# One more drain in GpSimd's program, ahead of the last expert's scatters

## The chip, the cores and the metric

The kernel runs on one core of one Trainium2 chip. The metric is device time in microseconds (us); lower is better. A core has five engines that run their own instruction streams: TensorE (PE; its weight loads are PEld), VectorE (DVE), ScalarE (ACT), GpSimd (POOL) and SyncE (SP). They meet only at semaphores. A "q" behind an engine's name (POOLq) marks instructions of its sequencer: waits, branches and drains. A drain is an instruction without data that stands in an engine's program and is meant to let what was issued before it finish; TensorE's at the close begins at 898.2 us in this trace, takes 4.27 us, and ends when the last matmul does, at 902.4.

## The reference

A token-shift layer whose channel mix goes through 16 experts; B = 8, T = 1024, D = 512, F = 1024, E = 16, N = 8192 tokens, C = 512 places for each expert.

```
xprev = concat([cond[:, None], x[:, :-1]], 1)
xk = x + (xprev - x) * maa_k ;  xr = x + (xprev - x) * maa_r
expert = token_id * 5099 % 16 ; pos = rank of the token within its expert
slot = expert * C + pos, tokens with pos >= C are dropped
h = relu(expert_in @ w_key[e]) ** 2 ;  y = h @ w_value[e]
out = x + sigmoid(xr @ w_recept) * y[slot]
```

## The kernel before

Phase 1 computes the gates sigmoid(xr @ w_recept) for 16 groups of 512 tokens and stores them to the DRAM tensor `gates`; beside it the routing is worked out: for each of the 64 tiles of 128 slots, which token stands in each row (`row_tok`), and the rows of the pairs (`row_pair`). Phase 2 goes through the 16 experts. For each, TensorE makes 8 tiles of the hidden layer (`up`, 4 steps of depth) and then 4 tiles of 128 rows of the result (`down`, 8 steps of depth). Each float32 product is made as three products of split operands (`triple`, lines 758 to 760). ScalarE and VectorE split, apply relu and square. VectorE closes each result tile t with two operations: `gate` = acc x mask x gate (line 682) and `xrow` = gate + xrow (line 685), which raises s_res.

GpSimd issues every indirect DMA, in an order written out by hand (lines 368 to 389). `gather_pairs(e)` fetches the inputs of expert e in 16 DMAs (line 348); `gather_gate` and `gather_cur` fetch for each tile the gate rows and the x rows (both through line 330); `scatter(e, t)` waits for s_res (line 354) and writes the tile's rows to `out` (line 355). In the loop over experts, the pairs of expert e + 2 come first, and then, for each tile, the scatter of expert e and the gathers of expert e + 1. For e = 14 there are no pairs left; its last instruction is the gather of x rows for tile 3 of expert 15 (line 387). For e = 15 only the four scatters remain. The loop at line 388 then waits until each tile's scatters have all landed. In all GpSimd issues 448 indirect DMAs. SyncE issues all other DMAs.

The block that holds the five programs closes at its end; the profile puts the instructions of this close under line 81. Each engine runs a drain there and then passes a meeting of semaphores with the others. These drains are not written in the kernel's text: they come with the block.

Of the kernel before, what the change touches and what calls it, by code (L numbers as in the profile page):

```python
# [23 lines left out]
def moe_token_shift(nc, x, pairs, xs_t, ids, maa_k, maa_r, w_recept_t, w_key, w_value, out, gates):  # L24
# [23 lines left out]
    E, D, F = w_key.shape  # L48
# [32 lines left out]
    with ExitStack() as ctx:  # L81
# [216 lines left out]
        def _(pool):  # L298
# [29 lines left out]
            def gather(table, e, t, rows, dst, s):  # L328
                a = e * ST + t
                pool.indirect_dma_start(dst, None, table,  # L330
                                        bass.IndirectOffsetOnAxis(rows[:, a:a + 1], 0)).then_inc(s, 16)

            def gather_cur(e, t):
                if e > 0:
                    pool.wait_ge(s_scat[t], 16 * e)
                gather(x, e, t, row_tok, xrow[:, t, :], s_cur[t])

            def gather_gate(e, t):
                if e > 0:
                    pool.wait_ge(s_res, (e - 1) * ST + t + 1)  # L340
                gather(gates, e, t, row_tok, gate[:, t, :], s_gat[t])

            def gather_pairs(e):
                if e >= 2:
                    pool.wait_ge(s_block, 2 * KD * (e - 1))
                for i in range(SB):
                    a = e * SB + i
                    pool.indirect_dma_start(pair[e % 2][:, i, :], None, pairs,  # L348
                                            bass.IndirectOffsetOnAxis(row_pair[:, a:a + 1], 0)).then_inc(
                                                s_pair[e % 2], 16)  # L350

            def scatter(e, t):
                a = e * ST + t
                pool.wait_ge(s_res, e * ST + t + 1)
                pool.indirect_dma_start(out, bass.IndirectOffsetOnAxis(row_tok[:, a:a + 1], 0),  # L355
                                        xrow[:, t, :], None).then_inc(s_scat[t], 16)
# [20 lines left out]
            for e in range(E):  # L377
                if e + 2 < E:
                    gather_pairs(e + 2)
                for t in range(ST):  # L380
                    scatter(e, t)
                    if e + 1 < E:
                        gather_gate(e + 1, t)
                        if t > 0:
                            gather_cur(e + 1, t - 1)
                if e + 1 < E:
                    gather_cur(e + 1, ST - 1)
            for t in range(ST):
                pool.wait_ge(s_scat[t], 16 * E)

# [501 lines left out]
```

## Time and profile before

| | |
|---|---|
| median of 3 runs | 918.49 us (917.84 to 919.08) |
| span of the profiled execution, first to last instruction | 916.6 us |
| the profiled execution's own time | not given beside the span |
| PE busy | 893.0 us (97%) |
| DVE busy | 775.1 us (85%) |
| POOL busy | 550.8 us (60%) |
| ACT busy | 380.0 us (41%) |
| granted TensorE clock, mean share of full speed | 0.988 |

Busy time is the sum of an engine's instructions; drains, waits and branches are not counted in it. The span is what one profiled execution shows; the median is from other executions.

### The profile page before, as it was taken

What the parts mean: (1) busy time and instruction counts of PE and PEld (TensorE: products, weight loads), DVE (VectorE), ACT (ScalarE), POOL (GpSimd) and SP (SyncE); (2) the same over time, 40 slices, a digit from 0 to 9 for tenths busy, and PEclk for the clock granted to TensorE, in tenths of its full rate; (3) what the DMA queues carried; (4) which work ended last, traced back from release to release, by engine and by line L of the source; (5) the groups of instructions that cost most, each with busy time, mean ns of one, the idle gap of its engine ahead of it and who ended that gap; (6) DMA issues with size and microseconds to landing.
All of it is one profiled execution on the core that took longest, in us unless ns stands there. A gap on an engine that the chain in (4) does not pass through costs nothing.

```text
span 916.6 us, 10890 instructions
## 1 busy us (share of the span) xinstructions
PE 893.0 (97%) x3915; PEld 735.4 (80%) x3915; DVE 775.1 (85%) x1060; ACT 380.0 (41%) x582; POOL 550.8 (60%) x485
## 2 busy tenths in 40 slices
PE   6999999999999999999999999999999999999993
PEld 5788878888888888888888888888888888888882
DVE  6999986878898989898989898989888898989841
ACT  4444322545352625353444444343525262535320
POOL 5222203576777777677767777677777676770601
PEclk9999988999999999999999999999999999999997
DMA  9555634866666666667585848485766667673600
GB/s 329 203 177 190 204 118 141 295 210 228 206 223 210 211 225 220 230 194 249 172 274 175 269 148 286 143 280 166 255 189 237 206 213 224 214 237 106 230 12 34
DMA packets 73765, 186.40 MB, mean 203 GB/s; under 512 B 11760, under 2 KB 11760, under 8 KB 73712
## 3 DMA queue, kind: packets, MB, share of 16 engines
q1 hardware_dynamic: 46064, 101.80, 34.0%
q0 software_dynamic: 27648, 83.91, 26.7%
q8 instruction: 31, 0.51, 0.2%
q14 instruction: 22, 0.18, 0.1%
HBM read 152.11 MB, written 33.55 MB: 203 GB/s over the span
## 4 chain that ended last, share of the span: by engine, by line
PE 94%; DVE 2%; issue 1%; DMA 0%; POOL 0%; ACT 0%; SPq 0%; DVEq 0%; POOLq 0%
PE acc L758 31%; PE acc L760 31%; PE acc L759 31%; PE rt_bank L792 2%; DVE xr_lo L636 1%; DMA wr_raw<-w_recept_t 0%; DVE mix L627 0%; DVE mix L630 0%; DVE cum L517 0%; POOL out L355 0%; DVE onehot L511 0%; DVE id_low L509 0%; DVE totals L521 0%; PE rt_bank L801 0%; DVE gate L682 0%
## 5 line engine op out<-in xcount | busy, mean ns | idle before, releaser
L758 PE MATMUL acc<-xk_hi,wk_hi 128*128 128x512 f32 x512 | 199.5, 390 | 0.0
L760 PE MATMUL acc<-xk_hi,wk_lo 128*128 128x512 f32 x512 | 199.4, 390 | 0.0
L759 PE MATMUL acc<-wv_lo,h_hi 128*128 128x512 f32 x512 | 199.3, 389 | 0.0
L760 PE MATMUL acc<-wv_hi,h_lo 128*128 128x512 f32 x512 | 199.2, 389 | 0.0
L758 PE MATMUL acc<-wv_hi,h_hi 128*128 128x512 f32 x512 | 199.2, 389 | 0.0
L759 PE MATMUL acc<-xk_lo,wk_hi 128*128 128x512 f32 x512 | 199.2, 389 | 0.0
L433 ACT ACTIVATE hid<-acc 128x512 f32<-128x512 f32 x128 | 76.6, 599 | 266.1 <-PE acc L760 266.1
L348 POOL DMA_INDIRECT pair_even<-pairs,row_pair x128 | 140.1, 1095 | 70.6 <-issue 38.7
L348 POOL DMA_INDIRECT pair_odd<-pairs,row_pair x128 | 140.1, 1095 | 46.6 <-issue 38.7
L355 POOL DMA_INDIRECT out<-xrow,row_tok x64 | 84.9, 1327 | 111.8 <-DVE xrow L685 102.1
L670 DVE TENSOR_TENSOR hid<-hid 128x512 f32<-128x512 f32 x128 | 88.4, 690 | 51.6 <-ACT hid L433 49.8
L760 PEld LDWEIGHTS acc<-xk_hi,wk_lo 128*128 128x128 f32 x512 | 96.1, 188 | 20.3
L759 PEld LDWEIGHTS acc<-xk_lo,wk_hi 128*128 128x128 f32 x512 | 96.1, 188 | 20.2
L758 PEld LDWEIGHTS acc<-wv_hi,h_hi 128*128 128x128 f32 x512 | 96.1, 188 | 20.0
L760 PEld LDWEIGHTS acc<-wv_hi,h_lo 128*128 128x128 f32 x512 | 96.1, 188 | 20.0
L758 PEld LDWEIGHTS acc<-xk_hi,wk_hi 128*128 128x128 f32 x512 | 96.1, 188 | 20.0
L759 PEld LDWEIGHTS acc<-wv_lo,h_hi 128*128 128x128 f32 x512 | 96.1, 188 | 20.0
L758 PE MATMUL acc<-wr_hi,xr_hi 128*128 128x512 f32 x256 | 101.8, 397 | 7.9 <-DVE xr_lo L636 7.9
L759 PE MATMUL acc<-wr_lo,xr_hi 128*128 128x512 f32 x256 | 101.1, 395 | 0.0
L760 PE MATMUL acc<-wr_hi,xr_lo 128*128 128x512 f32 x256 | 100.9, 394 | 0.0
L330 POOL DMA_INDIRECT xrow<-x,row_tok x64 | 79.5, 1242 | 21.2 <-issue 18.0
L674 DVE TENSOR_TENSOR h_lo<-hid,h_hi 128x512 fp32r<-128x512 f32 x128 | 87.9, 687 | 1.4
(105 smaller groups left out, 1259.1 us busy)
## 6 DMA issues: line engine op xcount, KB each, us to landing
raw<-w_key SPq DMA_DIRECT2D x64, 512.0 KB, 4.4
raw<-w_value SPq DMA_DIRECT2D x64, 512.0 KB, 3.9
xT<-xs_t SPq DMA_DIRECT2D x64, 256.5 KB, 4.0
gates<-gate SPq DMA_DIRECT2D x64, 256.0 KB, 2.8
pair_even<-pairs,row_pair POOLq DMA_INDIRECT x128, 3.3
pair_odd<-pairs,row_pair POOLq DMA_INDIRECT x128, 3.0
wr_raw<-w_recept_t SPq DMA_DIRECT2D x4, 256.0 KB, 5.0
xrow<-x,row_tok POOLq DMA_INDIRECT x64, 5.2
```

What stands on the lines that cost most here:

```text
L330: pool.indirect_dma_start(dst, None, table, bass.IndirectOffsetOnAxis(rows[:, a:a + 1], 0)).then_inc(s, 16)
L348: pool.indirect_dma_start(pair[e % 2][:, i, :], None, pairs, bass.IndirectOffsetOnAxis(row_pair[:, a:a + 1], 0)).then_inc(s_pair[e % 2], 16)
L355: pool.indirect_dma_start(out, bass.IndirectOffsetOnAxis(row_tok[:, a:a + 1], 0), xrow[:, t, :], None).then_inc(s_scat[t], 16)
L433: act.activation(hid[:, n % H_SLOTS, :], acc[n % 4][:, :], ACT.Relu).then_inc(s_relu, 1)
L636: dve.tensor_tensor(xr_lo[:, g % 2, k, :], mix[:, n % MIX_SLOTS, :], xr_hi[:, g % 2, k, :].bitcast(F32), ALU.subtract).then_inc(s_rlo, 1)
L670: dve.tensor_tensor(h, h, h, ALU.mult).then_inc(s_sq, 1)
L674: dve.tensor_tensor(h_lo[:, n % KF, :], hid[:, n % H_SLOTS, :], h_hi[:, n % KF, :].bitcast(F32), ALU.subtract).then_inc(s_hlo, 1)
L758: pe.matmul(bank[:, :], hi, m_hi, start=first, stop=False)
L759: pe.matmul(bank[:, :], hi, m_lo, start=False, stop=False)
L760: return pe.matmul(bank[:, :], lo, m_hi, start=False, stop=last)
L792: mm = pe.matmul(inv_ps[:, 0:2 * A], oh_b[:, :, j], oh_aw[:, :, :, j].rearrange("p h a -> p (h a)"), start=(j == 0), stop=(j == J - 1))
```

## The change

A drain is issued on GpSimd once, at the end of the loop's turn e = 14. It stands behind the gather of line 387 and ahead of the wait and the scatter of tile 0 of expert 15. Nothing else is changed.

```diff
                 if e + 1 < E:
                     gather_cur(e + 1, ST - 1)
+                if e + 2 == E:
+                    pool.drain()
             for t in range(ST):
                 pool.wait_ge(s_scat[t], 16 * E)
```

Blank lines of the diff are left out here; they put the drain on line 391 of the changed file.

## Rows read from the trace of the kernel before

**Rows 1.** The page: busy time with share and count, and the chain by engine.
```profile
PE 893.0 (97%) x3915; PEld 735.4 (80%) x3915; DVE 775.1 (85%) x1060; ACT 380.0 (41%) x582; POOL 550.8 (60%) x485
...
PE 94%; DVE 2%; issue 1%; DMA 0%; POOL 0%; ACT 0%; SPq 0%; DVEq 0%; POOLq 0%
```

**Rows 2.** Timeline, PE and DVE, 901.7 to the end: start us, us, what.
```profile
901.99 0.39 PE L760 MATMUL acc<-wv_hi,h_lo 128*128 128x512 f32 x1
...
902.41 0.75 DVE L682 SCALAR_TENSOR_TENSOR gate<-acc,mask,gate 128x512 f32<-128x512 f32 x1 [3.96 <-PE acc L760]
903.20 0.69 DVE L685 TENSOR_TENSOR xrow<-gate,xrow 128x512 f32<-128x512 f32 x1
```

**Rows 3.** Timeline, POOL, expert 15's scatters after the first; idle time in brackets.
```profile
893.29 0.99 POOL L355 DMA_INDIRECT out<-xrow,row_tok  x1 [4.45 <-DVE xrow L685]
898.73 0.97 POOL L355 DMA_INDIRECT out<-xrow,row_tok  x1 [4.46 <-DVE xrow L685]
904.17 0.97 POOL L355 DMA_INDIRECT out<-xrow,row_tok  x1 [4.47 <-DVE xrow L685]
```

**Rows 4.** Line 389: duration ns min/median/max, first and last start us.
```profile
L389 POOLq EVENT_SEMAPHORE  x2: 17/30/43, 903.9 to 906.9; - x2
```

**Rows 5.** Line 81, the block's close, same columns.
```profile
L81 POOLq EVENT_SEMAPHORE  x2: 17/17/17, 916.4 to 916.5; - x2
L81 SPq DRAIN  x1: 123/123/123, 864.8 to 864.8; - x1
L81 ACTq DRAIN  x1: 652/652/652, 882.0 to 882.0; - x1
L81 PEldq DRAIN  x1: 4267/4267/4267, 898.2 to 898.2; - x1
L81 DVEq DRAIN  x1: 730/730/730, 903.2 to 903.2; - x1
...
L81 POOLq DRAIN  x1: 9214/9214/9214, 907.2 to 907.2; - x1
L81 SPq EVENT_SEMAPHORE  x1: 17/17/17, 916.5 to 916.5; - x1
```

**Rows 6.** Busy us by stretch: PE, PEld, DVE, ACT, POOL, PEclk, DMA share, GB/s.
```profile
868.40:887.90 19.50, 19.50 (x87) 16.14 (x86) 11.62 (x16) 7.80 (x13) 0.10 (x2) 1.00 0.05 17
...
907.10:916.40 9.30, 0.00 (x0) 0.00 (x0) 0.00 (x0) 0.00 (x0) 0.00 (x0) 0.52 0.00 0
```

**Rows 7.** DMA in 907.2 to 916.4.
```profile
DMA packets 0, 0.00 MB, mean 0 GB/s; under 512 B 0, under 2 KB 0, under 8 KB 0
```

**Rows 8.** Line 884, the program's start, GpSimd: columns as in rows 4.
```profile
L884 POOLq DRAIN  x1: 188/188/188, 0.4 to 0.4; - x1
L884 POOL MEMSET const-uint8-127<- x1: 119/119/119, 0.4 to 0.4; 128x1 uint8 x1
```

**Rows 9.** Lines 348, 330 and 355: all indirect DMAs, and line 330's landings.
```profile
L348 POOL DMA_INDIRECT pair_even<-pairs,row_pair x128: 942/1028/1913, 149.0 to 759.1; - x128
L348 POOL DMA_INDIRECT pair_odd<-pairs,row_pair x128: 942/1027/1911, 184.7 to 803.9; - x128
...
L330 POOL DMA_INDIRECT xrow<-x,row_tok x64: 942/972/1795, 171.2 to 866.8; - x64
L330 POOL DMA_INDIRECT gate<-gates,row_tok x64: 944/1081/1209, 211.2 to 864.1; - x64
...
DMA to landing us min/median/max: 3.5/4.7/7.0
...
L355 POOL DMA_INDIRECT out<-xrow,row_tok x64: 966/1072/1730, 239.5 to 904.2; - x64
```

**Rows 10.** Timeline, POOL, around the place of the change.
```profile
865.54 0.95 POOL L330 DMA_INDIRECT xrow<-x,row_tok  x1 [0.30 <-issue]
866.80 1.66 POOL L330 DMA_INDIRECT xrow<-x,row_tok  x1 [0.30 <-issue]
887.85 0.99 POOL L355 DMA_INDIRECT out<-xrow,row_tok  x1 [19.40 <-DVE xrow L685]
```

## The prediction

> **What bounds the kernel now.** I read the busy times first, then the chain that ended last, then the ends of the engines. PE is busy 893.0 of 916.6 us, and the chain is 94% PE [rows 1]. So nothing in GpSimd's program matters until PE stops, unless it makes PE wait; what GpSimd does matters after PE's last product. The reader should therefore look at the last 15 us. The last matmul begins at 901.99, the last pair of VectorE operations runs from 902.41 to 903.89, and the last scatter is issued at 904.17 and takes 0.97 [rows 2, 3]. GpSimd's last wait, for that scatter's landing, is done at 906.9 [rows 4]. The span still ends only at 916.6.
>
> The program's end accounts for what is left. Every engine has a drain at line 81, where the block closes. Sync, ScalarE, TensorE and VectorE have begun theirs by 903.2, and the longest of these, TensorE's 4,267 ns from 898.2, ends at 902.4, with its last matmul. GpSimd's begins at 907.2 and takes 9,214 ns. The closing semaphore instructions start at 916.4 and 916.5, right behind it [rows 5]. All four others wait for GpSimd there, so these 9.21 us, 1.0% of the span, are the last thing on the path. They are no wait for transfers or compute: in 907.1 to 916.4 no engine is busy and the DMA share is 0.00 [rows 6], and in 907.2 to 916.4 the count of packets is 0 [rows 7]. So this drain does work of its own, on something GpSimd has piled up. The only other GpSimd drain in the trace, at 0.4 us, took 188 ns [rows 8]. It has memsets ahead of it and no indirect DMA; one such memset takes 119 ns [rows 8], so most of the 188 is a wait for it. Between the two drains lie 448 indirect DMAs (128 + 128 pair gathers, 64 + 64 row gathers, 64 scatters) [rows 9]. My reading is that a GpSimd drain has one piece of bookkeeping for each software DMA issued since the drain before: (9,214 - 188) / 448 = 20.1 ns each with a fixed 188, or 9,214 / 448 = 20.6 ns each with nothing fixed.
>
> **The change part by part.** One instruction is added, on GpSimd alone, when e is 14: after the last gather of the last expert (line 387) and ahead of the wait and scatter (lines 354 and 355) of tile 0 of expert 15. Nothing is removed or moved. There are four terms.
>
> 1. The added drain. It stands behind 444 of the 448 DMAs. I price it at 444 x 20.6 ns = 9.13 us. The trace has no drain of GpSimd in mid-program, so the bounds are 0.19 us (the early drain, rows 8) and 9.21 us (the late one, rows 5), plus at most a wait for the gathers still in flight. I take 9.13 because the place resembles the late drain in all but 4 DMAs. What hides it is GpSimd's idle time: its last gather is issued from 866.80 to 868.46, and the scatter behind it begins at 887.85, after 19.40 us of idle time that VectorE's xrow operation ended [rows 10]. Even if the drain first waits for the transfers in flight, these land by 7.0 us after issue at most [rows 9], which is 873.8, counted from the start of the issue; the drain then ends near 882.9, about 5 us before the scatter is due. During the gap the DMA share is 0.05 [rows 6]. Cost: 0.
>
> 2. What is queued behind it: only the four scatters and their final waits. The gathers that VectorE's results need were issued ahead of it, and PE and ScalarE wait for nothing that GpSimd still issues. If the cover were gone the scatters could still catch up. They are paced by PE, 5.44 us apart (887.85, 893.29, 898.73, 904.17), but one takes 0.97 to 0.99 and about 0.30 lies between issues [rows 3, 10]. Three go by in 3 x 1.29 = 3.9 us, so the first could start at 904.17 - 3.87 = 900.3 without moving the last. The real cover is 900.3 - 868.5 = 31.8 us, more than three times the price.
>
> 3. The final drain, now with 4 DMAs since the one before. By count alone it is 4 x 20.6 ns = 0.08 us; with the early drain's 188 ns as a fixed part, 0.27 us. The bounds are 0.08 and 9.21. I take 0.2, nearest to the early drain, because the scatters have landed and there is nothing else to wait for. It saves 9.21 - 0.2 = 9.01 us, all of it exposed. Behind it the 0.2 us of closing semaphores, 916.4 to 916.6, stays.
>
> 4. One more instruction to fetch and decode, in an idle engine: 0, bounded by the 0.30 us between two issues [rows 10], and it is under the same gap.
>
> In sum the span goes from 916.6 to 916.6 - 9.0 = 907.6. The profile gives the execution's span and no time beside it; the median of the three timed runs is 918.49, 1.89 us above. That difference lies around the span and stays. Forecast: 918.49 - 9.0 = 909.5 us, 0.98% faster. What is late next is the last product with its evict, scatter and landing, which no drain touches.
>
> A rule of the Trainium skill speaks against this. VectorE: DVE Perf Modes, section The DRAIN you can't avoid, says that besides VectorE's pipeline flush there are boilerplate drains in the preamble and postamble, constant at about 12 ns on all five engines. Priced so, the final drain would hold nothing to move, the added one would be free, and the time would stay 918.5. The trace disagrees for GpSimd: 188 and 9,214 ns [rows 5, 8]; Sync's 123 ns is no 12 ns either [rows 5].
>
> **The rivals.**
>
> A. A fixed price: a GpSimd drain costs about 9.2 us once the program has used software DMAs at all, whatever their number, as if it walked a table of fixed size. For it: the trace has only one such drain, and one point makes no line. Against it: nothing but the plainness of a count. The added drain is then hidden (868.5 + 9.2 = 877.7, before 887.85) and the final one stays 9.21: 918.5 us, no change. That the added drain doesn't do the same work as the one at the block's end, or that the work is tied to the program's end, gives the same time.
>
> B. Partly fixed: say half of the 9.21 is fixed, half goes by count. The final drain is then 4.6 + 0.0, the saving 4.6 us, and the time 913.9 us.
>
> C. Slower: in mid-program the drain handles each DMA at a much dearer price, because it must ask after each one while traffic is on. The place is GpSimd between 868.5 and the last scatter. At 100 ns each it takes 44.4 us and ends at 912.9; the last scatter starts 3.9 later, at 916.8 in place of 904.17, which is 12.6 us late, and with 9.0 saved at the end the time is 918.49 + 12.6 - 9.0 = 922.1 us. It decides from 31.8 + 9.0 = 40.8 us of drain, or 92 ns for each DMA, 4.5 times what the final drain shows. Against it: the gap is nearly without traffic [rows 6].
>
> **How the numbers follow.** Forecast 0.79, A 0.12, B 0.05, C 0.04. A measurement of this kernel tells 0.2%, 1.84 us, from no change. Faster: forecast and B, 0.84. Same: A, less a small part of it, 0.11. Slower: C and that part, a disturbance I don't see, 0.05. The forecast's own spread is 0.08 to 0.27 for the last drain and 0.6 us of the runs to either side (917.84 to 919.08): 908.8 to 910.2. The range reaches part of B: 908.5 to 913.0, which leaves out A, C and half of B, under 2 in 10.
>
> **What would show it.** In the profile after: a GpSimd drain at line 391 (the changed file's), from about 868.6 and 9.1 us long (5 us more if it waits for landings first); the drain at line 81 down from 9,214 to between 80 and 300 ns; scatters at unchanged times, 887.85 and so on; the chain up to the last landing unchanged; the span at 907.6. The forecast is wrong if the drain at line 81 stays at 9.2 us (A) or near 4.6 (B), or if the first scatter of expert 15 is released by the drain and not by VectorE (towards C). One thing the result alone can't tell: a cost that is paid once, by whichever drain comes first after a software DMA, gives the same time as a cost by count.

## The result, and the profile after

The changed kernel takes 910.12 us (median of 4 runs, 909.66 to 910.77) against 918.4 us before (median of 4 runs, 917.84 to 919.08). The ratio is 0.9908, 95% interval [0.9896, 0.992]: 0.92% faster. The forecast was 909.5. In experiments 1 to 4 and 9 to 12, further down, the chips granted TensorE a lower mean clock (0.949 to 0.989) and times ran up to 995 us, so of these only ratios of fast runs and the lengths of GpSimd's drains are compared.

The profile of one execution (909.74 us, of which 908.0 are the span) shows where it went. First the added drain at line 391 (the columns are duration in ns min/median/max, first and last start in us), then line 81, the block's close:

```profile
L391 POOLq DRAIN  x1: 11235/11235/11235, 866.4 to 866.4; - x1
```

```profile
L81 PEldq DRAIN  x1: 4267/4267/4267, 898.4 to 898.4; - x1
L81 DVEq DRAIN  x1: 732/732/732, 903.5 to 903.5; - x1
...
L81 POOLq DRAIN  x1: 383/383/383, 907.4 to 907.4; - x1
L81 SPq EVENT_SEMAPHORE  x1: 17/17/17, 908.0 to 908.0; - x1
```

The close of [rows 5] fell from 9,214 to 383 ns, 8.83 us. The timeline of GpSimd shows that the added drain delayed no scatter:

```profile
867.05 1.66 POOL L330 DMA_INDIRECT xrow<-x,row_tok  x1 [0.30 <-issue]
888.11 0.99 POOL L355 DMA_INDIRECT out<-xrow,row_tok  x1 [19.40 <-DVE xrow L689]
...
904.42 0.97 POOL L355 DMA_INDIRECT out<-xrow,row_tok  x1 [4.48 <-DVE xrow L689]
```

The gap of 19.40 us is the one of [rows 10] to the hundredth, and VectorE still ends it. The drain's own row needs care. It starts at 866.4, when the last gather has not begun (867.05), so 2.3 of its 11.2 us pass before that gather's issue has ended. It ends at 877.6, which is 8.9 us behind the end of the last gather's issue at 868.7 and 10.5 us ahead of the scatter.

The last scatter begins at 904.42 where it began at 904.17 [rows 3], so 8.83 - 0.25 = 8.58 us is what the span shows (916.6 to 908.0). Those 0.25 us come from earlier: the last matmul starts at 902.24 where it started at 901.99 [rows 2]. That looks like spread and not like the change: experiments 7 and 8 below hold the same drain, and there the last scatter begins at 903.95 and 904.56, to either side of both kernels.

### The profile page after: what moved, and what is told of

It reads as the page before. It is cut to its first block, busy times and chain, and to the rows that moved or that the text cites. A ratio compares the mean times of both kernels' runs of the same rounds, so it can differ in the third digit from the quotient of the medians.

```text
span 908.0 us, 10891 instructions
## 1 busy us (share of the span) xinstructions
PE 893.5 (98%) x3915; PEld 735.7 (81%) x3915; DVE 775.2 (85%) x1060; ACT 380.0 (42%) x582; POOL 549.4 (61%) x485
## 4 chain that ended last, share of the span: by engine, by line
PE 95%; DVE 2%; issue 1%; DMA 0%; POOL 0%; ACT 0%; SPq 0%; DVEq 0%; POOLq 0%
PE acc L762 31%; PE acc L764 31%; PE acc L763 31%; PE rt_bank L796 2%; DVE xr_lo L640 1%; DMA wr_raw<-w_recept_t 0%; DVE mix L631 0%; DVE mix L634 0%; DVE cum L521 0%; POOL out L355 0%; DVE onehot L515 0%; DVE id_low L513 0%; DVE totals L525 0%; PE rt_bank L805 0%; DVE gate L686 0%
```

## The experiments

What had to be told apart: my theory (work for each DMA since the last drain, here about 20 ns) from a cost that the first drain behind a software DMA pays once, and from a price that is partly fixed; then, whether the cover is what makes the added drain free. The lengths of GpSimd's drains hold from run to run: 383 ns came out twice, and the early drain of [rows 8] took 188 or 189 ns in every run. The edits of experiments 7, 8 and 12 are shown against the changed kernel, all others against the kernel before; blank lines are left out.

### 1 and 11. One drain, early

```diff
                     gather_cur(e + 1, ST - 1)
+                if e == 0:
+                    pool.drain()
```

> The changed kernel's two drains can be read in two ways: a cost by count, or a cost that the first drain behind a software DMA pays once. Here the only added drain stands at the end of e = 0, behind 68 DMAs, and 380 follow it. By count, with the line through the two measured closes (9,214 ns for 448 DMAs, 383 ns for 4: 19.9 ns each and 303 ns fixed), the added drain takes 68 x 19.9 + 303 = 1.66 us and the close 380 x 19.9 + 303 = 7.86 us; the time is 918.4 - 1.35 = 917.05 us. Paid once: the added drain takes about 9 us, the close 0.2 to 0.4, and the time is that of the changed kernel, 909.5 to 910. By a table of fixed size (rival A), already contradicted by the 383 ns: both 9.2 us, 918.4.

The close, in the first and in the repeated run:

```profile
L81 POOLq DRAIN  x1: 9203/9203/9203, 919.9 to 919.9; - x1
```

```profile
L81 POOLq DRAIN  x1: 9203/9203/9203, 933.0 to 933.0; - x1
```

The ratio to the kernel before is 0.9994 [0.9914, 1.0074]. A cost paid once is out: the close is as dear as without the drain. But so is my line of 19.9 ns: 380 DMAs cost what 448 do, to 11 ns. There is an upper limit of some kind; experiments 2, 9 and 10 show that it is a peak to which the cost returns. The repeat was for the time:

> The kernel with one drain at the end of e = 0 once more, to have its time to a few tenths of a per cent. In its first run the close took 9,203 ns behind 380 DMAs, 11 ns less than with 448. So no change: 918.4 to 918.7 us, within 0.2% of the kernel before. By the line of 19.9 ns each it would be 917.1; by a cost paid once, 910.

The repeat gave the length again, and no time that tells 0.2%: 944 to 991 us, beside 934 to 988 for the kernel before. Its time stays unmeasured; that the close is unchanged is shown.

### 2. One drain, half way

```diff
                     gather_cur(e + 1, ST - 1)
+                if e == 7:
+                    pool.drain()
```

> The only added drain stands at the end of e = 7, behind 40 + 8 x 28 = 264 DMAs; 184 follow it. By count: the close takes 184 x 19.9 + 303 = 3.96 us, the time is 918.4 - 5.25 = 913.15 us. Paid once: close 0.2 to 0.4 us, time 909.5 to 910. A half-fixed price (rival B) would leave the close near 4.6 + 1.9 = 6.5 us and the time near 915.7.

```profile
L81 POOLq DRAIN  x1: 6917/6917/6917, 929.2 to 929.2; - x1
```

6.92 us, where the line gives 3.96 and rival B 6.5. B looks right for a moment, but a fixed half can't be reconciled with the changed kernel's 383 ns for 4 DMAs. Ratio 0.9986 [0.9891, 1.0081]; the 2.3 us that the close lost are below what it tells.

### 3. Many drains

```diff
+            pool.drain()
             pool.wait_ge(s_rows, 1)
             gather_pairs(0)
...
                     scatter(e, t)
+                    if e == 15 and t == 2:
+                        pool.drain()
...
                     gather_cur(e + 1, ST - 1)
+                if e in (0, 2, 6, 13, 14):
+                    pool.drain()
+                if e == 14:
+                    pool.drain()
```

> Nine drains besides the close, each with another count since the one before: 0 DMAs behind GpSimd's 18 subtractions and the constants of phase 1; 68 at the end of e = 0; 56 at e = 2; 112 at e = 6; 196 at e = 13; 12 at e = 14 and 0 right behind it; 3 behind the third scatter of expert 15; 1 at the close. By count of DMAs, from the end of the last issue: 0.2 to 0.3 us for 0, then 1.66, 1.42, 2.53, 4.20, 0.54, 0.3, 0.36, and 0.32 for the close. By count of all instructions the first would take 36 x 19.9 ns more, about 1.0 us. If a drain waits until transfers in flight have landed, each in mid-program stays at least 3 to 7 us behind its last issue. The time: all of it in GpSimd's idle time, so that of the changed kernel, 910.1, within 0.6; slower if GpSimd, which runs ahead of VectorE by little at some of these places, delays a gather.

The rows of the drain behind phase 1's subtractions, of the second one at e = 14, and of the close:

```profile
L367 POOLq DRAIN  x1: 1456/1456/1456, 115.3 to 115.3; - x1
...
L394 POOLq DRAIN  x1: 53/53/53, 887.1 to 887.1; - x1
...
L81 POOLq DRAIN  x1: 128/128/128, 922.8 to 922.8; - x1
```

The first has only to outlast a subtraction that is issued at 115.32 and takes 1.36 us; it ends at 116.75, 0.07 us behind it. So compute instructions leave no work that shows, DMAs do. A drain right behind another takes 53 ns, and one DMA takes the close to 128 ns. The five drains at line 392 have gathers in flight in front of them and run from 3.0 to 9.2 us behind the last issue. For 12 DMAs it is 3.0 us (887.1 against 884.07, the end of the last issue). The trace's last landing update is at 886.56, 0.5 us before that drain's end; behind the third scatter, where 3 DMAs are counted, the last landing is at 917.05 and the drain ends at 917.21. So a short drain waits for the landing, and drains with transfers in flight are unfit for the law; hence experiments 9 and 10. The edit adds eight drains; the nine of the expectation take in the close. Ratio 0.9868 [0.9748, 0.9988]: they cost nothing that can be seen, though those at e = 0, 2 and 6 hold up the next pair gathers, which start 0.73 us behind the drain's end.

### 4. The changed kernel again

> The changed kernel again, for comparison on the same chip: 910.1 us, 0.991 of the kernel before; the drain at e = 14 ends 8.9 us behind the last gather's issue, the close takes 0.38 us, by every theory.

Ratio 0.9909 [0.9825, 0.9992], close 383 ns, and the added drain ends 8.89 us behind the last issue. The time in us was 928.43 on this chip.

### 5. The drain without its cover

```diff
                     scatter(e, t)
+                    if e == 15 and t == 2:
+                        pool.drain()
```

> The same one drain, moved out of its cover: it stands behind the third scatter of expert 15 and ahead of the fourth. 447 DMAs stand before it. If place and cover are what matters, it takes 447 x 19.9 = 8.9 us, plus up to 0.3, from the end of the third scatter's issue at 899.7, so to 908.6 to 908.9, and the fourth scatter starts there in place of 904.2, 4.4 to 4.7 us late; the close has one DMA and takes 0.32 us, 8.9 us less. Time 918.4 + 4.5 - 8.9 = 914.0 us. If a drain anywhere ahead of the close shortened the program as such: 910.

914.89 us against 918.71, ratio 0.9956 [0.9939, 0.9973], so 3.8 us of the 9 remain. GpSimd's timeline, and the close:

```profile
899.95 0.97 POOL L355 DMA_INDIRECT out<-xrow,row_tok  x1 [4.45 <-DVE xrow L687]
910.79 0.97 POOL L355 DMA_INDIRECT out<-xrow,row_tok  x1 [9.87 <-issue]
```

```profile
L81 POOLq DRAIN  x1: 138/138/138, 913.8 to 913.8; - x1
```

In place of "<-DVE xrow" stands "<-issue": nothing but the drain held the fourth scatter. By the spacing of 5.44 us it was due at 905.39 and began at 910.79, 5.4 late; 9.21 - 0.14 - 5.4 = 3.7 us, as timed. I had 4.5 late; the drain ended 9.1 us behind the issue and 0.7 more passed until the scatter, as it does in the other runs that have a ready DMA right behind a drain (0.73 to 0.76 us, once 1.05). What counts is the cover, not the drain.

### 6. The drain behind the last scatter

```diff
                     scatter(e, t)
+                    if e == 15 and t == 3:
+                        pool.drain()
```

> The drain stands behind the fourth scatter of expert 15, ahead of the waits for its landing. All 448 DMAs are before it and one of them is in flight. If the drain does its work by count while the last transfer flies, it runs from 905.1 to 905.1 + 8.9 = 914.0, the waits are then already met, the close takes 0.3 us, and the time is 918.4 - 9.2 + (914.0 - 907.0) + 0.3 = 916.5 us: 1.9 us faster, the flight of the last scatter. If a drain first waits for the landing (906.9) and then does its count, the time is 918.4 plus 0.3, no change.

917.26 us against 918.71, ratio 0.9983 [0.9974, 0.9993]. The scatter, the drain, and the wait behind it:

```profile
905.04 0.97 POOL L355 DMA_INDIRECT out<-xrow,row_tok  x1 [4.47 <-DVE xrow L687]
...
L383 POOLq DRAIN  x1: 10427/10427/10427, 904.8 to 904.8; - x1
...
L391 POOLq EVENT_SEMAPHORE  x2: 17/30/43, 915.3 to 915.3; - x2
...
L81 POOLq DRAIN  x1: 43/43/43, 915.6 to 915.6; - x1
```

The drain ends at 915.23, 9.22 us behind the end of the issue (906.01), as long as the close before with everything landed. That transfer lands at 907.76 in this trace. Had the drain first waited for it, the work of 9.2 us would have ended near 917.0. So the work on the old DMAs goes on while the last transfer flies, and hides it: 1.9 us by the expectation, 1.45 by the medians. With no DMA behind a drain the close takes 43 ns.

### 7 and 8. What is counted: DMAs or rows

```diff
                 if e + 2 == E:
                     pool.drain()
+                    pool.wait_ge(s_block, 2 * KD * E)
+                    for i in range(12):
+                        pool.indirect_dma_start(
+                            pair[1][:, i, :], None, pairs,
+                            bass.IndirectOffsetOnAxis(row_pair[:, i:i + 1], 0)).then_inc(s_pair[1], 16)
```

and a wait for them at the end. Experiment 8 has `0:16` in place of `:` for the partitions.

> The changed kernel with 12 more pair gathers of 128 rows behind the added drain, into pair_odd, whose last contents have been read; their data are not used. They fill GpSimd's idle time, and the four scatters follow. The close has 16 DMAs since the drain, each over 128 partitions. By count of DMAs: 303 + 16 x 19.9 = 0.62 us. Time: 12 x 1.3 = 15.6 us of issues from about 878 to 893.5 make the first scatters late but not the fourth, so about 910.4.

> The same with 12 gathers of 16 rows each, an eighth of the descriptors. What does a drain count? If DMA instructions, the close takes 0.62 us as with 128 rows. If rows or packets, the 12 count as 1.5 full ones: 303 + 5.5 x 19.9 = 0.41 us. Time about 910.4 by both.

The closes, of 128 rows and of 16 rows:

```profile
L81 POOLq DRAIN  x1: 1363/1363/1363, 907.0 to 907.0; - x1
```

```profile
L81 POOLq DRAIN  x1: 1358/1358/1358, 907.7 to 907.7; - x1
```

An eighth of the rows changes 5 ns of 1,363. It counts DMA instructions. But 16 of them cost 1.36 us and not 0.62: (1,363 - 383) / 12 = 82 ns each. The times of one run each were 910.38 and 910.97 us. In experiment 7 the extra issues end at 893.6 and the first scatter starts at 893.93. By the spacing of 5.44 us it was due at 903.95 - 16.32 = 887.63, so it is 6.3 us late, while the fourth starts at 903.95 on VectorE's release: the scatters catch up, as the prediction's second term has it.

### 9 and 10. The law, with nothing in flight

```diff
+                if e in (0, 3, 7, 12, 13):
+                    if e + 2 < E:
+                        pool.wait_ge(s_pair[e % 2], 16 * SB * (e // 2 + 2))
+                    for t in range(ST):
+                        pool.wait_ge(s_scat[t], 16 * (e + 1))
+                        pool.wait_ge(s_gat[t], 16 * (e + 2))
+                        pool.wait_ge(s_cur[t], 16 * (e + 2))
+                    pool.drain()
```

Experiment 10 has `(2, 8)` for the list.

> Six drains with nothing in flight: GpSimd first waits until all its own DMAs have landed. Since the drain before, 68 DMAs at e = 0, 84 at e = 3, 112 at e = 7, 140 at e = 12, 28 at e = 13, 16 at the close. The closes measured so far (43 ns for 0, 128 and 138 for 1, 383 for 4, 1,363 and 1,358 for 16, 6,917 for 184, 9,203 for 380, 9,214 for 448) fit 43 + 82.5 n for few DMAs and a ceiling near 9.2 us, about 111 entries, for many. By that law: 5.65, 6.97, 9.2, something from 6.9 to 9.2 (past the ceiling it seems to fall back in steps), 2.35 and 1.36 us. By the line of 19.9 ns each that I drew earlier: 1.66, 1.97, 2.53, 3.09, 0.86, 0.62. The time: no claim within 1 us; about 910 to 912.

> Two such drains past the ceiling: 124 DMAs at e = 2, 168 at e = 8, and the close with 212. If the number of entries kept simply stops at about 111, all three take 9.2 us. If the issuing of a DMA throws out finished entries in batches once the store is full, they lie between 6.9 and 9.2 us and the value depends on where in a batch the drain falls; 184 gave 6.92. By the first line (303 + 19.9 n): 2.8, 3.6 and 4.5.

The drains of experiment 9, in order of time, behind 68, 84, 112, 140 and 28 DMAs, and its close behind 16:

```profile
L395 POOLq DRAIN  x1: 5618/5618/5618, 286.4 to 286.4; - x1
L395 POOLq DRAIN  x1: 6907/6907/6907, 424.6 to 424.6; - x1
L395 POOLq DRAIN  x1: 9184/9184/9184, 608.6 to 608.6; - x1
L395 POOLq DRAIN  x1: 3304/3304/3304, 837.4 to 837.4; - x1
L395 POOLq DRAIN  x1: 2324/2324/2324, 889.0 to 889.0; - x1
...
L81 POOLq DRAIN  x1: 1347/1347/1347, 955.9 to 955.9; - x1
```

Those of experiment 10, behind 124 and 168, and its close behind 156:

```profile
L395 POOLq DRAIN  x1: 3332/3332/3332, 375.5 to 375.5; - x1
L395 POOLq DRAIN  x1: 5601/5601/5601, 643.1 to 643.1; - x1
...
L81 POOLq DRAIN  x1: 4614/4614/4614, 944.3 to 944.3; - x1
```

The expectation of experiment 10 had 212 DMAs for its close by a slip; 448 - 124 - 168 is 156. Past 112 DMAs I had expected 6.9 to 9.2 us, and that failed: these drains take 3.3 to 5.6. I call the 82 ns of work for one DMA an entry; that is a name for what the lengths show, no run looks inside. With (9,184 - 43) / 112 = 81.6 ns an entry, the drains with all DMAs landed give nearly whole numbers of entries:

| DMAs since the last drain | ns | (ns - 43) / 81.6 |
|---|---|---|
| 0 | 43 | 0 |
| 1 | 128 to 138 | 1.0 to 1.2 |
| 4 | 383 | 4.2 |
| 16 | 1,347 to 1,363 | 16.0 to 16.2 |
| 28 | 2,324 | 28.0 |
| 68 | 5,618 | 68.3 |
| 84 | 6,907 | 84.1 |
| 112 | 9,184 | 112 (sets the rate) |
| 124 | 3,332 | 40.3 |
| 140 | 3,304 | 40.0 |
| 156 | 4,614 | 56.0 |
| 168 | 5,601 | 68.1 |
| 184 | 6,917 | 84.2 |
| 380 | 9,203 | 112.3 |
| 448 | 9,214 | 112.4 |

Up to 112 the drain handles one entry for each DMA, at 82 ns. Elapsed time isn't what is counted: 16 DMAs took 1,363 ns 30 us behind the drain before (experiment 7) and 1,347 ns 65 us behind it (experiment 9). Between 112 and 124 entries fall away without a drain: 84 of them in one case (124 leaves 40), 100 in the others (140, 156, 168, 184); past that the number rises by one for each DMA again. The cost is a sawtooth. 448 = 112 + 4 x 84 and 380 = 112 + 100 + 2 x 84 fit this with the peak just reached, and four drains with transfers in flight fit it too, counted from the end of the last issue: 448 DMAs took 9,221 ns (experiment 6), 447 took 9,141, one entry less (experiment 5), 444 took 8,895, four entries less (the changed kernel), and 196 took 7,892 ns, 96 entries, which is 196 - 100 (experiment 3). In these runs 84 fall away where one counts from the program's start, and 100 the first time behind an earlier drain; why is open. That the issue of a DMA throws out finished entries when a store is full is my reading; no run shows it. No single issue pays 82 ns for each of them, since the longest issue of all runs took 2.0 us. Whether the peak of 112 counts DMAs or something that is alike for all DMAs of this kernel is open too, and was not tried.

### 12. The changed kernel and one drain more

```diff
                     scatter(e, t)
+                    if e == 15 and t == 2:
+                        pool.drain()
```

> The changed kernel with a second drain behind the third scatter of expert 15: the close then has one DMA since the last drain and takes 0.13 us in place of 0.38. The second drain, behind 3 DMAs, ends about 1.9 us behind the issue, at 901.9, before the fourth scatter at 904.4. The time should be 0.25 us below the changed kernel's, 909.9, which a time can't tell and the length of the close can.

```profile
925.34 0.97 POOL L355 DMA_INDIRECT out<-xrow,row_tok  x1 [4.46 <-DVE xrow L691]
930.77 0.97 POOL L355 DMA_INDIRECT out<-xrow,row_tok  x1 [4.47 <-DVE xrow L691]
...
L81 POOLq DRAIN  x1: 128/128/128, 933.8 to 933.8; - x1
```

The close is 0.25 us shorter, and the fourth scatter is still released by VectorE. That this version is faster than the changed kernel is argued from the close and not timed: the runs took 935 to 989 us, and the changed kernel did not run beside them.

## Why the prediction was right

- **Where the 9.2 us sit and that they can be moved**: right. The span's end is held by GpSimd's own work on DMAs that have long landed, the drain in mid-program does the same work (8.9 us behind the last issue), and the close keeps only what came since. The rule of about 12 ns from the Trainium skill (VectorE: DVE Perf Modes, section The DRAIN you can't avoid) agrees with more of the trace than the prediction says: at the program's start, line 884, the other four engines' drains take 7 to 10 ns. It holds neither for GpSimd's 188 ns there nor for any drain of the close: 123 ns for Sync, up to 4,267 for TensorE, and 43 to 9,214 for GpSimd in the various runs; whether the page means the close's drains at all is not clear from its words.
- **The cover** (first and second term): right, and shown from both sides. The 19.40 us gap is untouched, the scatters catch up when the first is 6.3 us late (experiment 7), and where the cover is missing 5.4 us are lost (experiment 5). The fear that the drain first waits for landings didn't come true for 444 to 448 DMAs; short drains do wait, and in between it adds something: behind 56 and 68 DMAs with transfers in flight, experiments 1, 3 and 11 show 6.0 to 6.5 us where the count gives 4.6 and 5.6, and behind 264 (experiment 2) 8.7 where it gives 7.9.
- **The price of the added drain**: 9.13 forecast, 8.9 measured, but by a wrong law, and so by luck. I divided 9.21 us by 448 DMAs. The rate is 82 ns, four times that, and only 112 entries were there to be paid for. The forecast price came out because a drain of 444 lies as near the peak as one of 448: (8,895 - 43) / 81.6 is 108.5, and 444 - 4 x 84 is 108.
- **The final drain** (third term): the mis-sized one. 0.2 forecast, 0.38 measured, outside my 0.08 to 0.27: 4 x 82 + 43 ns. It is 0.18 of the 0.4 us by which the span (908.0 for 907.6) missed; the rest is the 0.25 us by which everything up to the last scatter came later. The time missed by 0.6 us, where the four runs spread over 1.1.
- **The rivals**. A, no change, was wrong as a whole and right in one thing that I had waved off: the cost is bounded, at 9.2 us, however many DMAs the program holds. B is out by 383 ns. C is out: it decides from 40.8 us of drain, and 8.9 were measured. Its 92 ns for each DMA is near the true rate of 82, and 444 of them at 82 ns, 36.4 us, would have run beyond the cover of 31.8; what kept the drain short is that only some 108 were left to pay, not that one is cheap. The once-paid cost, which I said the result couldn't tell from mine, is out by experiment 1.

The place also mattered more than I knew. At e = 0 the same instruction gives nothing back, at e = 7 2.3 us of the 9.2, since 380 and 184 DMAs behind the drain bring the cost back to 9.2 and 6.9 us. The size of the gain is this kernel's own, too: its 448 DMAs happen to end on a peak of the sawtooth, and by the table a close behind 124 or 140 DMAs would have had 3.3 us to give back.

## What to carry to other kernels

Read the end of the trace behind the last landing: on an engine that issues many indirect DMAs, the drain at the block's close can be the last thing on the path. A drain in that engine's last idle stretch, as late as the stretch allows and before the last few DMAs, moves the cost under other work; here it needed 8.9 us of idle time, and all but 43 ns and 82 ns for each of the 4 DMAs that follow was given back. One point of a cost (9,214 ns for 448) gives no rate: vary the count before dividing.

## What the hardware showed that I had not expected

- A GpSimd drain with all DMAs landed takes 43 ns and 82 ns for each DMA since the last drain (0 to 112 of them), whether the DMA moved 128 rows or 16 (1,363 and 1,358 ns).
- The cost tops out at 112 entries, 9.2 us, and past it falls back to 3.3 us (124 and 140 DMAs) before it rises again: a sawtooth, so more DMAs can mean a cheaper drain.
- With transfers in flight a drain at the peak is no longer (9.22 us for 448, 9.20 for 112); behind 56 DMAs it took 6.4 us where the count gives 4.6, and behind 12 it waited for the landing (3.0 us).
- A mid-program drain's row can start up to 2.6 us before the issue of the DMA ahead of it ends (2.3 in the changed kernel): read its end, not its length.
- A DMA that is ready right behind a drain starts 0.73 to 0.76 us behind its end (experiments 1 to 3, 5 and 7 to 11; once 1.05, in experiment 10), against 0.30 us between two issues.
